# Score tiles made in pairs and one unit further ahead, in heads 1 to 7 of a first attention on TensorE

## The chip, the cores and the metric

The kernel runs on one core of a Trainium2 chip. The metric is the device time of one launch in microseconds (us). It is one fused program of two transformer blocks; the change is in the first block's attention.

## The reference, cut to what matters

```python
x = x + _L0_xattn_ref(ctx_768, _layernorm(x), mask, ...)   # the part of this case
x = x + _L0_ffn_ref(_layernorm(x), ...)
x = x + _L1_xattn_ref(_layernorm(x), ctx_768, ...)
x = x + _L1_ffn_ref(_layernorm(x), ...)                    # mixture of 8 experts
# x: 2 x 1024 x 256; context: 2 x 77 x 192; 4 heads of 64

def _L0_xattn_ref(x, latents, mask, ...):
    xn = layernorm(x); ln = layernorm(latents)
    q = ln @ Wq.T
    kv = concatenate([xn @ Wkv.T, ln @ Wlkv.T], axis=1)    # 77 + 1024 keys
    qn = rmsnorm(q) * SCALE; kn = rmsnorm(k)               # by heads
    attn = where(full_mask, einsum('bhid,bhjd->bhij', qn, kn), -max)
    out = einsum('bhij,bhjd->bhid', softmax(attn), v)
    return out @ Wo.T + bo
```

For each of 2 batches and 4 heads the scores are 1024 queries by 1101 keys, followed by a softmax over the keys, the product with the values, and the output product with Wo, which is added into x.

## The kernel before

Each engine has a program of its own, a list in fixed order written out by Python generators; semaphores are the only tie between them. The eight pairs of batch and head are heads 0 to 7. `attention(hi)` (L570) walks one head in 18 units, 9 tiles of keys (eight of 128 and one of 77) for each half of 512 queries.

For unit u TensorE makes the tile of scores (called qk here, L600 and L601: two matmuls in fp32r, the second one adding the low part and the row of maxima) in PSUM bank 4 or 5 by turns. ScalarE takes exp of it into PT[u % 4] (L1865). One unit later TensorE multiplies that by the values (pv, L583, an fp32 product that the trace shows as two matmuls) into bank 6 or 7, summed over the nine units of a half.

The softmax needs the maximum of each row first. It is made one head ahead: `max_tile(hi + 1, qt)` (L540) multiplies 128 queries by all keys into banks 0 to 2 (L547, three matmuls), and VectorE reduces all three banks to a column (L1227). After four such columns `max_row` turns them (L555), ScalarE negates them (mrt) and a DMA writes them as a row of QB. In heads 1 to 6 a max_tile stands at the end of each even unit up to 14.

The output product is made one head behind: `wo_tile(hi - 1, qt)` (L558) multiplies OT by Wo into one of banks 0 to 2, `qt % 3` (L444, which is the line of the helper `three`), and VectorE divides by the row sum (L1232) and adds into x (L1235). It stands at the end of each odd unit up to 15. Head 7 has no max_tile, only wo_tile.

`busy[m]` holds for each bank the semaphore value that frees it, and `clear(m)` waits for that. A max_tile clears banks 0, 1 and 2, so it waits for the VectorE work on the wo_tile ahead of it; a wo_tile's bank is freed by the reduction of the max_tile ahead of it. A score bank is freed by the exponential of the tile in it (`a_exp`).

After each unit the main loop (`merge`, L43) puts in side work of other stages, 1.0 or 1.4 steps a unit: query and key projections with their squares (ACT qkr, sq), transposes of a head's queries and keys (L524; ScalarE copies QA, or KA and KB; VectorE makes QB and the low half of KA), transposes of layer norms (L453), and in head 7 four small products for the feed-forward weights (L635; VectorE tsp, ScalarE w1e). These have their place in every engine's list: on ScalarE the side work after unit u - 1 comes behind exp(u - 1) and ahead of exp(u). Nothing of ScalarE's, VectorE's, GpSimd's or SyncE's lists is touched by the change. At unit 9 ScalarE and VectorE also copy the first half's result out of bank 6 (OT).

Of the kernel before, what the change touches and what calls it, by code (L numbers as in the profile page):

```python
# [82 lines left out]
def build(nc, A, out, y_dram):  # L83
    with ExitStack() as root:
# [341 lines left out]
        def tensor_program(pe):  # L426

            busy = [None] * 8
            at = {"unit": 0}
# [5 lines left out]
            def clear(b):  # L435
                if busy[b]:
                    pe.wait_ge(*busy[b])
                    busy[b] = None
# [101 lines left out]
            def max_tile(hi, qt):  # L540
                h = hi % H0
                for j in range(3):
                    clear(j)
                if qt == 0:
                    pe.wait_ge(v_ka, 2 * hi + 2)
                for j in range(3):
                    op = pe.matmul(ps[:, j, 0:368], QA[:, h, 128 * qt:128 * qt + 128], KA[:, h, 368 * j:368 * j + 368],  # L547
                                   start=True, stop=True)
                    busy[j] = (v_mx, 8 * hi + qt + 1)
                op.then_inc(p_mx, 1)  # L550

            def max_row(hi, hf):
                clear(0)
                pe.wait_ge(v_mx, 8 * hi + 4 * hf + 4)
                pe.transpose(ps[0:4, 0, 0:128], mx[:, hi % 2, 4 * hf:4 * hf + 4], ident[:, :]).then_inc(p_mT, 1)  # L555
                busy[0] = (a_mrt, 2 * hi + hf + 1)

            def wo_tile(hi, qt):  # L558
                h, m = hi % H0, qt % 3
                c = slice(128 * qt, 128 * qt + 128)  # L560
                clear(m)
                if qt % 4 == 0:
                    pe.wait_ge(v_ot, 2 * hi + qt // 4 + 1)
                if hi == 0 and qt == 0:
                    pe.wait_ge(a_whi, 3)
                    pe.wait_ge(g_wlo, 3)
                three(bank[m][:, 0:258], [((OT[0][:, c], OT[1][:, c]), (wo[0][:, h, :], wo[1][:, h, :]))]).then_inc(p_wo, 1)
                busy[m] = (v_x, 8 * hi + qt + 1)

            def attention(hi):  # L570
                b, h = HEADS[hi]
                units = [(hf, kt) for hf in range(2) for kt in range(9)]

                def pv(u):
                    hf, kt = units[u]
                    K = 128 if kt < 8 else SC
                    if kt == 0:
                        clear(6 + hf)
                    pe.wait_ge(a_exp, 18 * hi + u + 1)
                    if hf == 0 and kt == 0 and h == 0:  # L580
                        pe.wait_ge(a_v if b else v_v, 8)
                        pe.wait_ge(a_vc, b + 1)
                    pe.matmul(bank[6 + hf][0:65, :], VA[b][0:K, kt, h, :], PT[u % 4][0:K, :], start=kt == 0,  # L583
                              stop=kt == 8).then_inc(p_pv, 1)
                    if kt == 8:
                        busy[6 + hf] = (v_ot, 2 * hi + hf + 1)

                if hi == 0:
                    pe.wait_ge(g_init, 6)
                for u, (hf, kt) in enumerate(units):  # L590
                    at["unit"] = u
                    K = 128 if kt < 8 else SC
                    ks, qc = slice(128 * kt, 128 * kt + K), slice(512 * hf, 512 * hf + 512)
                    m = 4 + u % 2
                    clear(m)
                    if u == 0:
                        pe.wait_ge(v_ka, 2 * hi + 2)
                    if kt == 0:
                        pe.wait_ge(d_mrow[2 * (hi % 2) + hf], 16 * (hi // 2 + 1))
                    pe.matmul(bank[m][0:K, :], KA[:, h, ks], QA[:, h, qc], start=True, stop=False)  # L600
                    pe.matmul(bank[m][0:K, :], KB[:, h, ks], QB[:, h, qc], start=False, stop=True).then_inc(p_s, 1)  # L601
                    busy[m] = (a_exp, 18 * hi + u + 1)
                    if u:
                        pv(u - 1)
                    if hi == 0 and u < 4:
                        max_tile(0, 4 + u)
                    if hi == 0 and u == 6:
                        max_row(0, 1)
                    when = MAX_AT if hi == 0 else range(0, 16, 2)
                    if hi < 7 and u in when:  # L610
                        max_tile(hi + 1, when.index(u))
                    if hi < 7 and u == (11 if hi == 0 else 9):
                        max_row(hi + 1, 0)
                    if hi < 7 and u == 17:
                        max_row(hi + 1, 1)
                    if hi and u % 2 and u < 16:
                        wo_tile(hi - 1, u // 2)
                    yield
                pv(17)
                at["unit"] = 0  # L620
# [273 lines left out]
            for hi in range(8):  # L894
                merge(attention(hi), (beside[hi], SIDE_RATE[hi]))
                drain(beside[hi])
# [1761 lines left out]
```

## Time and profile before

| | us |
|---|---|
| median of 3 runs | 895.92 |
| lowest, highest | 895.44, 902.13 |
| profiled execution | 889.07 |
| its span, first to last instruction | 887.3 |
| TensorE busy in it | 767.5 (86%) |
| VectorE busy | 547.5 (62%) |
| ScalarE busy | 395.9 (45%) |
| granted TensorE clock, mean | 0.951 |

The profiled execution is one run of its own, a little faster than the median of the timed runs; times of single instructions are from it. Matmuls are pipelined and their ends are modelled, so the distance from one start to the next says more than a matmul's duration.

### The profile page before, as it was taken

How to read it: one execution, taken by the hardware profiler on the slowest of the kernel's cores; microseconds unless marked ns; L12 is line 12 of the kernel's file. 1: busy time of each engine (PE TensorE's matmuls, PEld its weight loads, DVE VectorE, ACT ScalarE, POOL GpSimd, SP SyncE). 2: the span in 40 equal slices, each digit the busy share in tenths (PEclk: the TensorE clock that was granted, in tenths of full speed). 3: DMA queues.
4: the chain of work that ended last, by engine and by line, in shares of the span. 5: the costliest groups of instructions: out<-in, count | busy, mean ns of one | idle time of the engine just before them, and what ended most of it. 6: DMA issues, size and time to landing. Idle time of an engine off the chain costs nothing.

```text
span 887.3 us, 12600 instructions
## 1 busy us (share of the span) xinstructions
PE 767.5 (86%) x4724; PEld 612.5 (69%) x4724; DVE 547.5 (62%) x1140; ACT 395.9 (45%) x713; POOL 346.2 (39%) x311
## 2 busy tenths in 40 slices
PE   2748998998999999997999998998128999999996
PEld 2636554665565545565977988887018999999996
DVE  5666676566477667336643349886755676765642
ACT  2324543445344433556264124443206655676562
POOL 5414200320040011215543014333422888888873
PEclk9958999999999999999999999999558999999999
DMA  6000000000000010010002020112111443455432
GB/s 177 1 0 1 1 0 1 1 1 0 2 1 1 1 48 3 1 47 2 2 1 91 1 96 1 49 49 95 48 66 30 125 120 78 108 144 141 133 38 25
DMA packets 20110, 38.38 MB, mean 43 GB/s; under 512 B 4507, under 2 KB 15633, under 8 KB 17745
## 3 DMA queue, kind: packets, MB, share of 16 engines
q1 hardware_dynamic: 13393, 29.14, 9.8%
q0 software_dynamic: 6656, 8.43, 5.3%
q8 instruction: 38, 0.62, 0.3%
q14 instruction: 23, 0.19, 0.1%
HBM read 29.02 MB, written 8.40 MB: 42 GB/s over the span
## 4 chain that ended last, share of the span: by engine, by line
PE 64%; DVE 22%; issue 5%; ACT 5%; POOL 2%; DMA 1%; ACTq 0%; DVEq 0%; POOLq 0%
PE ps L444 19%; PE ps L1060 11%; PE ps L583 9%; PE ps L683 5%; DVE mx L1227 4%; PE ps L547 3%; PE ps L600 3%; PE ps L601 2%; DVE qkn L1186 2%; PE ps L524 2%; DVE rep L1614 1%; DVE sm L1426 1%; ACT htmp L1923 1%; PE ps L453 1%; DVE Pb L1430 1%
## 5 line engine op out<-in xcount | busy, mean ns | idle before, releaser
L583 PE MATMUL ps<-PT,VA 128*65 128x512 f32 (+1 forms) x288 | 147.5, 594 | 0.2 <-ACT PT L1865 0.2
L1865 ACT ACTIVATE PT<-ps 128x512 f32<-128x512 f32 x128 | 76.0, 594 | 65.9 <-PE ps L601 65.3
L1227 DVE TENSOR_REDUCE mx<-ps 128x1 f32<-128x1104 f32 x64 | 83.5, 1304 | 34.2 <-PE ps L547 33.9
L1060 PE MATMUL ps<-he,wh 128*128 128x258 f32 x768 | 104.0, 288 | 0.0
L444 PE MATMUL ps<-GT,wh 128*128 128x258 f32 x768 | 98.0, 287 | 1.1 <-DVE GT L1703 1.1
L444 PEld LDWEIGHTS ps<-GT,wh 128*128 128x128 f32 x768 | 94.8, 192 | 1.5 <-issue 1.5
L1060 PEld LDWEIGHTS ps<-he,wh 128*128 128x128 f32 x768 | 95.4, 189 | 0.4
L2192 POOL TENSOR_TENSOR rs<-rs,half 128x4 f32<-128x4 f32 (+2 forms) x19 | 17.8, 938 | 157.5 <-DVE rs L1100 126.8
L1733 DVE TENSOR_TENSOR he<-het,he 128x516 fp32r<-128x516 f32 x64 | 44.6, 697 | 53.6 <-ACT he L1757 53.1
L2201 POOL TENSOR_TENSOR ssq<-ssq,half 128x4 f32<-128x4 f32 x32 | 32.5, 1017 | 110.8 <-DVE ssq L1168 110.6
L2466 POOL DMA_INDIRECT out_dram<-ye,idx x40 | 62.3, 1557 | 24.2 <-DVE ye L1715 14.3
L547 PE MATMUL ps<-KA,QA 128*128 128x368 f32 x192 | 61.6, 431 | 11.3 <-DVE mx L1227 3.8
L600 PE MATMUL ps<-QA,KA 128*128 128x512 f32 x144 | 68.8, 478 | 1.4 <-DMA QB<-mrt 1.4
L547 PEld LDWEIGHTS ps<-KA,QA 128*128 128x128 f32 x192 | 35.2, 198 | 46.0 <-issue 30.2
L601 PE MATMUL ps<-QB,KB 65*128 65x512 f32 x144 | 57.5, 399 | 0.0
L444 PEld LDWEIGHTS ps<-wo,OT 65*128 65x128 f32 x192 | 29.2, 189 | 40.8 <-DVE mx L1227 31.8
L583 PEld LDWEIGHTS ps<-PT,VA 128*65 128x65 f32 (+1 forms) x288 | 39.1, 138 | 24.5 <-ACT PT L1865 4.4
L2348 POOL DMA_INDIRECT gt<-y_dram,idx x40 | 41.6, 1040 | 36.6 <-DVE gate L1693 25.0
L2140 ACT ACTIVATE het<-ps,b1e 128x516 f32<-128x516 f32 x64 | 44.4, 693 | 24.5 <-PE ps L444 21.3
L683 PE MATMUL ps<-w2e,hT 128*128 128x256 f32 x384 | 51.9, 291 | 2.1 <-ACT htmp L1923 2.1
L444 PE MATMUL ps<-xt,w1e 128*128 128x512 f32 x192 | 49.7, 410 | 3.9 <-ACT htmp L1923 3.8
L683 PEld LDWEIGHTS ps<-w2e,hT 128*128 128x128 f32 x384 | 48.1, 194 | 3.9 <-ACT htmp L1923 3.0
(264 smaller groups left out, 1535.5 us busy)
## 6 DMA issues: line engine op xcount, KB each, us to landing
wr<-in_w1e_dram SPq DMA_DIRECT2D x8, 1024.0 KB, 4.8
wr<-in_w2e_dram SPq DMA_DIRECT2D x8, 1024.0 KB, 7.7
x<-in_x_dram SPq DMA_DIRECT2D x4, 512.0 KB, 7.0
w<-in_w_dram SPq DMA_DIRECT2D x2, 1024.0 KB, 4.6
y_dram<-yr SPq DMA_DIRECT2D x3, 512.0 KB, 3.0
out_dram<-x SPq DMA_DIRECT2D x3, 512.0 KB, 4.1
gt<-y_dram,idx POOLq DMA_INDIRECT x40, 3.0
out_dram<-ye,idx POOLq DMA_INDIRECT x40, 4.7
```

Source lines behind the costliest of these rows:

```text
L444: op = pe.matmul(o, l, r, start=n == 0, stop=n == len(calls) - 1)
L547: op = pe.matmul(ps[:, j, 0:368], QA[:, h, 128 * qt:128 * qt + 128], KA[:, h, 368 * j:368 * j + 368], start=True, stop=True)
L583: pe.matmul(bank[6 + hf][0:65, :], VA[b][0:K, kt, h, :], PT[u % 4][0:K, :], start=kt == 0, stop=kt == 8).then_inc(p_pv, 1)
L600: pe.matmul(bank[m][0:K, :], KA[:, h, ks], QA[:, h, qc], start=True, stop=False)
L601: pe.matmul(bank[m][0:K, :], KB[:, h, ks], QB[:, h, qc], start=False, stop=True).then_inc(p_s, 1)
L683: op = pe.matmul(bank[bk][:, 0:256], l, r, start=n == 0, stop=n == 23)
L1060: op = pe.matmul(bank[dc][:, 0:258], w2h[i][:, wc_], he[j][:, m, 258 * c:258 * c + 258], start=n == 0, stop=n == 23)
L1227: v.tensor_reduce(mx[:, hi % 2, qt:qt + 1], ps[:, 0:3, 0:368], AX.XY, ALU.max).then_inc(v_mx, 1)
L1733: v.tensor_tensor(he[1][:, m, :], het[m % 2][:, :], f(he[0][:, m, :]), ALU.subtract).then_inc(v_he, 1)
L1865: a.activation(PT[u % 4][0:K, :], bank[4 + u % 2][0:K, :], ACT.Exp, bias=0.0 if K == 128 else mcol[:, b:b + 1]).then_inc(a_exp, 1)
L2140: a.activation(het[m % 2][:, :].rearrange("p (c n) -> p c n", c=2), ps[:, bp:bp + 2, 0:258], ACT.Gelu, bias=b1e[:, ex, m:m + 1]).then_inc( ...
L2466: g_.indirect_dma_start(out, bass.IndirectOffsetOnAxis(ap=idx[0:M, ex, s_:s_ + 1], axis=0), ye[ex % 2][0:M, s_, :], None, compute_op=ALU.a ...
```

## The change

In heads 1 to 7 the tiles of scores are made two at a time. Tiles 0 and 1 are made at unit 0; in each odd unit up to 15, after pv of the unit before, come tiles u + 1 and u + 2. The order in an even unit was qk(u), pv(u - 1), max_tile and is pv(u - 1), max_tile; in an odd unit it was qk(u), pv(u - 1), wo_tile and is pv(u - 1), qk(u + 1), qk(u + 2), wo_tile. Head 0 keeps its order. The same matmuls run with the same operands and banks; only their places in TensorE's list change, and with them the places of the waits for the score banks.

```diff
-                for u, (hf, kt) in enumerate(units):
-                    at["unit"] = u
+                def qk(u):
+                    hf, kt = units[u]
                     K = 128 if kt < 8 else SC
...
                     busy[m] = (a_exp, 18 * hi + u + 1)
+
+                for u in range(18):
+                    at["unit"] = u
+                    if hi == 0:
+                        qk(u)
+                    elif u == 0:
+                        qk(0)
+                        qk(1)
                     if u:
                         pv(u - 1)
+                    if hi and u % 2 and u < 17:
+
+                        qk(u + 1)
+                        qk(u + 2)
                     if hi == 0 and u < 4:
                         max_tile(0, 4 + u)
```

## Rows read from the trace of the kernel before

**Rows 1.** The page: the first line.

```profile
span 887.3 us, 12600 instructions
```

**Rows 2.** Windows of heads 5 and 7: busy by engine (instructions), granted clock, DMA.

```profile
283.27:319.00 35.73, 35.00 (x141) 19.72 (x140) 20.78 (x36) 15.69 (x29) 0.00 (x0) 1.00 0.00 1
...
356.50:386.26 29.76, 29.60 (x106) 15.48 (x105) 9.23 (x22) 14.00 (x24) 5.11 (x4) 1.00 0.00 1
```

**Rows 3.** Waits from 66 to 387 us: us in total, times, longest.

```profile
PEld ps L444 <- DVE mx L1227: 31.8, 39, 2.2
...
PEld ps L583 <- ACT PT L1865: 4.4, 9, 0.8
```

**Rows 4.** Timeline of a plain pair in head 5: start, duration, instruction, [idle before].

```profile
297.43 0.74 PE L547 MATMUL ps<-KA,QA 128*128 128x368 f32 x3
...
298.01 0.39 PE L600 MATMUL ps<-QA,KA 128*128 128x512 f32 x1
...
298.20 1.31 DVE L1227 TENSOR_REDUCE mx<-ps 128x1 f32<-128x1104 f32 x1 [0.93 <-PE ps L547]
...
298.46 1.02 PE L583 MATMUL ps<-PT,VA 128*65 128x512 f32 x2
...
299.57 0.63 PE L444 MATMUL ps<-wo,OT 65*128 65x258 f32 x3
...
300.43 0.48 DVE L1235 SCALAR_TENSOR_TENSOR x<-ps,rec,x 128x256 f32<-128x256 f32 x1
300.51 1.02 PE L583 MATMUL ps<-PT,VA 128*65 128x512 f32 x2
...
300.97 1.07 PE L547 MATMUL ps<-KA,QA 128*128 128x368 f32 x3
...
301.88 0.39 PE L600 MATMUL ps<-QA,KA 128*128 128x512 f32 x1
...
302.34 1.02 PE L583 MATMUL ps<-PT,VA 77*65 77x512 f32 x2
```

**Rows 5.** Timeline of TensorE in head 7, one pair without side work.

```profile
368.42 1.02 PE L583 MATMUL ps<-PT,VA 128*65 128x512 f32 x2
...
369.75 1.02 PE L583 MATMUL ps<-PT,VA 128*65 128x512 f32 x2
...
370.97 0.39 PE L600 MATMUL ps<-QA,KA 128*77 128x512 f32 x1
...
371.43 1.02 PE L583 MATMUL ps<-PT,VA 128*65 128x512 f32 x2
```

**Rows 6.** Timeline of head 4 after unit 12: transposes of keys and their copies.

```profile
272.88 0.60 PE L524 MATMUL ps<-ident,qkn 128*128 128x128 f32 x4
...
273.51 0.69 ACT L1757 ACTIVATE KA<-ps,gg 128x512 fp32r<-128x512 f32 x1 [1.20 <-PE ps L524]
...
274.67 0.58 ACT L1865 ACTIVATE PT<-ps 128x512 f32<-128x512 f32 x1
...
276.46 0.78 PE L547 MATMUL ps<-KA,QA 128*128 128x368 f32 x3
```

**Rows 7.** Timeline of head 7, units 1 and 2, with side products.

```profile
358.92 0.92 PE L444 MATMUL ps<-wo,OT 65*128 65x258 f32 x3
...
359.76 0.50 PE L635 MATMUL ps<-lrow 3*128 3x256 f32 x2
...
361.79 0.58 ACT L1865 ACTIVATE PT<-ps 128x512 f32<-128x512 f32 x1
```

**Rows 8.** Timeline of head 5, unit 9 and the maximum's product after it.

```profile
303.55 0.60 PE L444 MATMUL ps<-wo,OT 65*128 65x258 f32 x3
...
305.41 0.75 PE L547 MATMUL ps<-KA,QA 128*128 128x368 f32 x3
```

**Rows 9.** Timeline of TensorE: two waits for other work, in heads 2 and 3.

```profile
183.12 0.97 PE L444 MATMUL ps<-wv,xt 128*128 128x256 f32 x6 [0.93 <-DVE OT L1241]
...
206.37 0.74 PE L547 MATMUL ps<-KA,QA 128*128 128x368 f32 x3 [0.90 <-DVE KA L1203]
```

## The prediction

> **What bounds the kernel now.** I read the windows by head first, then the waits of the first attention, then the timeline in order of time. The whole execution spans 887.3 us [rows 1] and was timed at 889.07 us, so 1.8 us lie outside the span. The change touches only heads 1 to 7 of the first attention, from 111.42 to 386.26 us of it. TensorE is the bound there, but not tight: head 5 takes 35.73 us and head 7, which makes no maxima for a later head, 29.76 us, both at a granted clock of 1.00 [rows 2]. What TensorE loses has a name: the output product (L444 of wo_tile) stands 31.8 us in 39 cases with its weight queue on the maximum (L1227) [rows 3]. That figure counts the idle weight loader, which begins long before the matmuls in front of it end, so it is no price of the wait. I take the price from one pair of units.
>
> A plain pair of head 7 has two output-of-softmax products (pv), two score tiles (qk) and one wo tile and takes 371.43 - 368.42 = 3.01 us; pv plus qk is 369.75 - 368.42 = 1.33, qk is 371.43 - 370.97 = 0.46, so pv is 0.87 and wo 3.01 - 2.66 = 0.35 [rows 5]. A plain pair of head 5 has a maximum's product more, which takes 298.01 - 297.43 = 0.58 when its bank wait is exposed and about 0.51 when not (301.88 less the end of the pv begun at 300.51) [rows 4]. So the work is 3.01 + 0.51 = 3.52 us. The pair takes 302.34 - 298.46 = 3.88 [rows 4]. The waits are thus 0.36 us a pair: the pv of 298.46 ends at 299.33, wo starts at 299.57, just after the maximum of 298.20 + 1.31 = 299.51 (0.24); the rest is its exposed weight load.
>
> Two round trips between TensorE and VectorE share banks 0 to 2 and form a ring. A, from the start of the maximum's product to the start of wo: 299.57 - 297.43 = 2.14. B, from the start of wo to the next maximum's product, which needs all three banks and so the residual add (L1235) that ends at 300.91: 300.97 - 299.57 = 1.40 [rows 4]. A + B = 3.54 cannot be undercut by any order on TensorE.
>
> **The change part by part.** *Plain pairs.* Before, both trips were covered by one qk and one pv. After, A holds pv and two qk, B only pv. A needs 0.58 + 0.87 + 0.92 = 2.37 on TensorE, more than 2.14, so the wait for the maximum goes. B has 0.35 + 0.87 = 1.22 against 1.40: a new wait of 0.18 for the residual add, on the next max_tile. The pair takes 2.37 + 1.40 = 3.77, a gain of 0.11. I count 15 pairs of this kind in the timeline (heads 1, 3, 5, 6): 1.6 us gained. What is queued behind the new wait on TensorE is the maximum's product, then pv; ScalarE's exponentials are already made and are not delayed.
>
> *The pairs at unit 9* (heads 3, 5, 6). There the residual add also stands behind the VectorE half of OT, so that B is 305.41 - 303.55 = 1.86 [rows 8], 0.18 more than the 0.35 + 0.46 + 0.87 = 1.68 that TensorE has to do in it. The two tiles now lie between pv(8) and wo, so OT is through before wo ends and B is 1.40 as elsewhere: 0.11 + 0.18, near 0.28 a pair, x 3 = 0.8 gained.
>
> *Waits from outside.* The maximum's product of head 3's first unit waits 0.90 for the keys, and a value projection 0.93 for OT [rows 9]. A score tile that was behind these waits is now before them, worth 0.46 each; two pairs of heads 2 and 4 whose wo waited 0.24 have side work in B and lose nothing there. Together 0.92 + 0.48 = 1.4 gained.
>
> *Exponentials behind side work.* This is the other side of the ledger. qk(u+2) overwrites the bank of qk(u) and so waits for exp(u). Before, a tile never waited for its bank: the pv in front of it had waited for the same exponential, and that had two qk and more in front of it (it falls short by 4.4 us in 9 cases, again by the weight loader) [rows 3]. Now exp(u) for odd u must be ready one pv and one qk after the side work of u - 1. ScalarE runs in order, and when that side work is a head's keys it copies twice before it takes the exponential. From the transposes at 272.88 the copies start at 273.51 and the exponential ends at 274.67 + 0.58 = 275.25, 2.42 after the transposes [rows 6]. TensorE has 0.35 (transposes) + 0.87 + 0.46 = 1.68 to do until then: a wait of 0.8 before the second tile. Keys fall after an even unit three times (unit 4 of heads 3 and 5, unit 12 of head 4); in head 4 the next maximum's product stood late anyway (276.46), which takes a third off. Sum 2.1 lost. After an odd unit the keys' chain also delays the maximum on VectorE, so that pv(u+1) waits 0.7 but wo comes only 0.1 to 0.2 later: four cases, 0.6. A single copy or a projection's copy and square leave 0.05 to 0.1 each, 9 cases, 0.7 lost.
>
> *Head 7.* Its units 0 to 3 carry side products whose result goes over VectorE (tsp) and ScalarE (w1e) before the next exponential. From wo at 358.92 (its matmuls run from 359.33, after the pv) the exponential of unit 2 ends at 361.79 + 0.58 = 362.37, 3.04 later [rows 7]. Before, TensorE had wo, side, qk, pv, side, qk: 0.35 + 0.35 + 0.46 + 0.87 + 0.35 + 0.46 = 2.84, nearly all of it. After, wo, side, pv, side: 1.92, a wait of 1.1. The same after unit 3 without the second side product gives 1.5, and the tile after unit 0's side waits 0.75. That is 3.35; before, the covers of 2.84 and, after unit 3, 2.49 fell short of 3.04 too, by 0.2 and 0.55, so 2.6 are lost anew. The rest of head 7 has no wait before and gets none. If the side results came 1 us sooner, no more than 0.8 would be lost.
>
> Instructions added: none. The unit 0 of the next head has its row from the DMA some ten units early, and qk(9), now made at unit 7, needs a row sent at unit 17 of the head before; no queue is passed.
>
> Sum: -1.6 - 0.8 - 1.4 + 2.1 + 0.6 + 0.7 + 2.6 = +2.2 us against the profiled execution's 889.07, which is 891.3. The median of the three runs is 895.92; by ratio (1.0025) that becomes 898.2.
>
> A rule weighed: the row shows the exponential of the keys' unit 2.42 us after the transposes, against 1.68 us of cover [rows 6]. The Trainium skill, Perfetto Trace Analysis, "Matmuls", says that independent groups should rotate through different PSUM banks so that one is emptied while the next is made; two tiles back to back over only two banks leave that rotation. By it every pair would pay; by the rows only those with side work on ScalarE do, since in a plain pair the exponential ends over 1 us before its bank is wanted.
>
> **The rivals.** *The wait goes and nothing takes its place.* If the residual add came back faster than 1.40, all 0.36 of 18 pairs would go (6.5), and the outside waits 1.4: about 888. For it: the change aims at just this wait, the largest of TensorE's here [rows 3]. Against: B is the end of a matmul, a reciprocal and an add of 0.48 us in a row, which the change doesn't touch, and the cover of 1.22 is counted from the same rows [rows 4, 5].
>
> *Exponentials bind everywhere that side work is* (the slower side). Its place is the second tile's bank wait, its price up to 0.8 for each of the ten double copies of keys in heads 1 to 5, and 2.6 in head 7; it decides once ScalarE's in-order side copy ends later than one pv and one qk after its product. That is 8 + 2.6 + 1.3 less the 3.8 gained: +8, and with each projection's copy at 0.15 more, +10: 906. For it: ScalarE's queue is strictly ordered in the rows [rows 6, 7]. Against: half of the copies fall on odd units, where VectorE's chain hides them.
>
> *It does nothing:* VectorE's own chains (norms, the products that scale queries and keys) set most of the odd pairs, and gains and losses cancel: 896.
>
> *The clock falls.* The granted clock is 1.00 in these heads in spite of idle stretches [rows 2]; waits of 1.5 us in head 7 are new. At half clock for the first third of that head it would take about 10 us more: 908. The Trainium skill, TensorE: Matmul & The Clock Gate, "A second HAM failure mode", tells of a kernel whose short idles between groups made the clock oscillate; no row of this stretch shows that.
>
> **How the numbers follow.** Forecast (a few us slower, mostly given back) 0.66; exponentials bind 0.13; the wait simply goes 0.11; nothing 0.08; clock 0.02. A change of 1% (9 us) is about what a measurement of this kernel can tell, its three runs lying 6.7 us apart. The range of the forecast alone is 893 to 903: B between 1.22 and 1.45, and keys' waits between 0.3 and 1.0. To the rivals it is 888 to 906. Faster by over 1% needs more than the whole of the first rival: 0.07. Slower by over 1% is the upper part of the second and the clock: 0.11. Within 1%: 0.82.
>
> **What would show it.** Right: the weight loader's wait of L444 for L1227 shrinks to a third, that of L547 for L1235 grows to over 5 us; plain pairs of head 5 at 3.77; a new wait of L600 for an exponential in heads 3, 4, 5, 7; head 7 near 32 us, heads 3 to 6 within 1 us of before. Wrong: plain pairs at 3.55 (first rival), a wait before every second tile (second), or head 7 unchanged, which would take away my largest loss and leave the kernel at 896 or below.

## The result, and the profile after

The changed kernel takes 904.30 us, median of 20 runs (901.76 to 913.81); the kernel before 898.01 us, median of 20 (892.04 to 906.77; the three runs known before the prediction are among them). The ratio is 1.0101 with a 95% interval of 1.0078 to 1.0124: about 9 us slower. The ratio leaves out three slow, disturbed runs, all of the kernel before, and mostly for that reason is larger than the distance of the two medians (6.3 us). The profiled execution after took 903.53 us, that of before 889.07.

The page of the changed kernel, first line and granted clock in 40 slices:

```profile
span 901.7 us, 12600 instructions
...
PEclk9968999799999999999999999999558999999999
```

No instruction was added. I cut the span at the turning of the maxima (L555) in unit 17 of each head, which both kernels have, and measured from one to the next; head 7 ends at the first matmul of the experts. Times in us, with the clock where it is not 1.00:

| stretch | before | after | difference |
|---|---|---|---|
| start to head 0's turning | 110.85 (0.89) | 114.02 (0.88) | +3.2 |
| head 1 | 40.24 | 41.05 | +0.8 |
| head 2 | 52.35 | 56.59 (0.91) | +4.2 |
| head 3 | 37.07 | 36.71 | -0.4 |
| head 4 | 42.19 | 44.26 | +2.1 |
| head 5 | 35.72 | 35.59 | -0.1 |
| head 6 | 37.50 | 36.65 | -0.9 |
| head 7 | 30.34 | 32.59 | +2.2 |
| rest (experts and so on) | 501.04 (0.94) | 504.24 (0.94) | +3.2 |

The two outer stretches hold none of the change, since head 0 keeps its order, and they differ as much between executions of one order: over the twelve experiments below the first is 110.8 to 114.8 and the last 499.7 to 513.8. They are left out of the account, which is therefore one of the heads alone. The changed heads cost 8.0 us: 4.2 in head 2, 4.3 in heads 4 and 7, 0.8 in head 1, less 1.3 in heads 3, 5 and 6.

The heads of the changed kernel as windows (busy by engine with instructions, granted clock, DMA), heads 2, 4, 5 and 7; the last two answer to [rows 2]:

```profile
155.07:211.66 56.59, 52.12 (x238) 34.53 (x237) 31.06 (x59) 21.94 (x54) 13.74 (x13) 0.91 0.00 1
...
248.37:292.63 44.26, 40.76 (x189) 25.89 (x187) 30.83 (x54) 19.50 (x44) 11.87 (x10) 1.00 0.00 1
292.63:328.22 35.59, 34.66 (x141) 20.22 (x140) 20.95 (x36) 14.87 (x28) 0.00 (x0) 1.00 0.00 1
...
364.87:397.46 32.59, 30.19 (x109) 15.93 (x107) 9.39 (x22) 13.45 (x25) 5.11 (x4) 1.00 0.00 1
```

Head 2 is the only head with a clock under 1.00, and it is the largest loss. Where in it? The timeline of TensorE, changed kernel, around the end of head 1 (start, duration, instruction, [idle before]):

```profile
153.36 1.88 PE L583 MATMUL ps<-PT,VA 128*65 128x512 f32 x4
155.07 0.27 PE L555 MATMUL ps<-ident,mx 128*4 128x128 f32 x1
156.87 0.26 PE L469 MATMUL ps<-ident,yb 77*128 77x77 f32 x1 [1.52 <-DVE yb L1153]
156.96 0.23 PE L470 MATMUL ps<-ident,yb 77*64 77x77 f32 x1
157.63 1.99 PE L475 MATMUL ps<-wc,ctxT 128*77 128x512 f32 x2 [0.44 <-ACT ctxT L1769]
159.55 1.99 PE L476 MATMUL ps<-wc,ctxT 64*77 64x512 f32 x2
161.46 1.97 PE L583 MATMUL ps<-PT,VA 77*65 77x512 f32 x2
```

and the same place in the kernel before:

```profile
152.14 0.26 PE L469 MATMUL ps<-ident,yb 77*128 77x77 f32 x1 [0.78 <-DVE yb L1141]
...
152.90 1.08 PE L475 MATMUL ps<-wc,ctxT 128*77 128x512 f32 x2 [0.44 <-ACT ctxT L1757]
153.91 1.08 PE L476 MATMUL ps<-wc,ctxT 64*77 64x512 f32 x2
154.92 1.07 PE L583 MATMUL ps<-PT,VA 77*65 77x512 f32 x2
```

Here TensorE turns (transposes) the second batch item's normalised context (yb) and multiplies it into keys and values. The norm comes from VectorE, whose program the change does not touch. Before, units 16 and 17 still had a tile of scores each to put in front of it; now both tiles were made at unit 15, only pv products are left, and the wait is 1.52 us, not 0.78. From L475 on the same matmuls take nearly twice as long: the engine stood, did 0.3 us of small transposes, stood again, and then had its clock halved. In windows of 6 us the changed kernel reads

```profile
149.00:155.00 6.00, 5.98 (x25) 3.16 (x24) 4.76 (x11) 3.82 (x6) 0.02 (x1) 1.00 0.00 0
155.00:161.00 6.00, 4.05 (x8) 0.83 (x6) 1.08 (x3) 0.61 (x3) 0.53 (x1) 0.71 0.00 0
161.00:167.00 6.00, 6.00 (x16) 4.00 (x16) 2.51 (x5) 1.84 (x4) 1.40 (x2) 0.50 0.01 3
167.00:173.00 6.00, 6.00 (x33) 4.53 (x33) 2.75 (x6) 2.41 (x7) 1.01 (x1) 0.93 0.00 0
```

0.50 is the 1.2 GHz level, 1.00 the 2.4 GHz level; 6 us at 0.50 hold 16 instructions, and 6 us just behind hold 33. Before, the windows from 152 to 164 us are at 1.00. The wait itself costs 0.7 us and the clock some 4.

The waits of the weight loader in the first attention after (us in total, times, longest), which answer to [rows 3]:

```profile
PEld ps L600 <- ACT PT L1877: 11.3, 28, 1.0
PEld ps L547 <- DVE x L1247: 11.1, 17, 1.9
PEld ps L583 <- ACT PT L1877: 8.6, 11, 2.0
...
PEld ps L444 <- DVE mx L1239: 2.4, 5, 1.4
```

### The profile page after: what moved, and what is told of

Read it like the earlier page. It is cut to its first block, busy times and chain, and to the rows that moved or that the text cites. A ratio compares the mean times of both kernels' runs of the same rounds, so it can differ in the third digit from the quotient of the medians.

```text
span 901.7 us, 12600 instructions
## 1 busy us (share of the span) xinstructions
PE 774.2 (86%) x4724; PEld 617.3 (68%) x4724; DVE 551.2 (61%) x1140; ACT 390.9 (43%) x713; POOL 346.8 (38%) x311
## 4 chain that ended last, share of the span: by engine, by line
PE 65%; DVE 20%; ACT 6%; issue 5%; POOL 2%; DMA 1%; another core or an unknown queue 0%; ACTq 0%; DVEq 0%; POOLq 0%
PE ps L444 19%; PE ps L583 10%; PE ps L1072 9%; PE ps L695 5%; PE ps L547 4%; PE ps L600 3%; PE ps L601 3%; DVE qkn L1198 2%; DVE mx L1239 2%; PE ps L524 2%; DVE rep L1626 1%; DVE yb L1116 1%; DVE sm L1438 1%; ACT htmp L1935 1%; PE ps L453 1%
## 5 line engine op out<-in xcount | busy, mean ns | idle before, releaser
L444 PE MATMUL ps<-GT,wh 128*128 128x258 f32 x768 | 97.9, 287 | 1.1 <-DVE GT L1715 1.1
L444 PEld LDWEIGHTS ps<-GT,wh 128*128 128x128 f32 x768 | 94.7, 192 | 1.5 <-issue 1.5
L600 PE MATMUL ps<-QA,KA 128*128 128x512 f32 x144 | 86.3, 599 | 3.5 <-ACT PT L1877 2.0
L1877 ACT ACTIVATE PT<-ps 128x512 f32<-128x512 f32 x128 | 72.8, 591 | 36.7 <-PE ps L601 36.6
L547 PEld LDWEIGHTS ps<-KA,QA 128*128 128x128 f32 x192 | 34.6, 201 | 51.8 <-issue 27.4
L547 PE MATMUL ps<-KA,QA 128*128 128x368 f32 x192 | 57.8, 411 | 12.9 <-DVE x L1247 4.6
L444 PE MATMUL ps<-xt,w1e 128*128 128x512 f32 x192 | 49.9, 411 | 4.2 <-ACT htmp L1935 4.2
L583 PEld LDWEIGHTS ps<-PT,VA 128*65 128x65 f32 (+1 forms) x288 | 36.8, 139 | 21.2 <-issue 9.3
L600 PEld LDWEIGHTS ps<-QA,KA 128*128 128x128 f32 x144 | 27.0, 188 | 32.3 <-issue 18.7
```

Source lines behind the costliest of these rows:

```text
L444: op = pe.matmul(o, l, r, start=n == 0, stop=n == len(calls) - 1)
L1877: a.activation(PT[u % 4][0:K, :], bank[4 + u % 2][0:K, :], ACT.Exp, bias=0.0 if K == 128 else mcol[:, b:b + 1]).then_inc(a_exp, 1)
```

## Experiments

Twelve kernels ran, in four groups (1 to 4, 5 to 7, 8 to 10, 11 and 12). Each ratio is to the kernel before as timed in the same group; its own median moved between 891.0 and 900.3 us from group to group, so only ratios are compared across groups. The heads (from turning to turning, as above) in each one's profiled execution, in us, and where the granted clock was below 1.00:

| kernel | h1 | h2 | h3 | h4 | h5 | h6 | h7 |
|---|---|---|---|---|---|---|---|
| before | 40.24 | 52.35 | 37.07 | 42.19 | 35.72 | 37.50 | 30.34 |
| after | 41.05 | 56.59 (.91) | 36.71 | 44.26 | 35.59 | 36.65 | 32.59 |
| 1 head1_old | 40.23 | 52.02 | 36.68 | 44.31 | 35.63 | 36.60 | 32.56 |
| 2 filler_ctx | 41.05 | 52.71 | 36.65 | 44.31 | 35.64 | 36.61 | 35.76 (.90) |
| 3 before_tail1 | 40.23 | 56.84 (.91) | 37.07 | 42.19 | 35.73 | 37.55 | 30.33 |
| 4 pairs_again | 41.05 | 56.57 (.91) | 36.67 | 44.25 | 35.65 | 36.68 | 32.57 |
| 5 head7_old | 41.06 | 52.75 | 36.67 | 44.27 | 35.63 | 38.15 (.96) | 30.33 |
| 6 one_ahead | 40.02 | 54.42 (.94) | 36.61 | 42.65 | 35.51 | 37.05 | 30.95 |
| 7 chosen_heads | 40.22 | 52.03 | 36.04 | 45.23 (.96) | 34.66 | 38.14 (.96) | 30.31 |
| 8 chosen_2 | 40.23 | 52.01 | 36.02 | 42.16 | 34.66 | 37.05 | 30.33 |
| 9 chosen_2_filled | 40.23 | 51.92 | 36.02 | 42.17 | 34.66 | 37.06 | 30.32 |
| 10 before_filled | 40.26 | 52.30 | 37.07 | 42.19 | 35.66 | 37.52 | 30.35 |
| 11 tail1_again | 40.28 | 56.79 (.91) | 37.07 | 42.19 | 35.68 | 37.53 | 30.34 |
| 12 tail1_filled | 40.27 | 53.04 | 37.07 | 42.18 | 35.67 | 37.45 | 30.34 |

At full clock one order gives the same head within 0.1 us in every execution, so a head's own cost can be read from a single profile.

**1. head1_old: head 1 keeps the old order.**

```diff
-                    if hi == 0:
+                    if hi in (0, 1):
...
-                    if hi and u % 2 and u < 17:
+                    if not (hi in (0, 1)) and u % 2 and u < 17:
```

> The changed kernel, but head 1 keeps the old order (as head 0 does). Theory (tail and clock): in the changed kernel TensorE has no score tiles left to do while VectorE and GpSimd prepare the context's key projection at the end of head 1; it stands 1.5 us, and the granted clock is at half until some 10 us later. With head 1 in the old order the clock stays at 1.00 between heads 1 and 2 and the stretch from the turning of the last maxima of head 0's successor (L555) to that of head 2 returns to the 52.4 us of before: 3.5 to 5.5 us faster than the changed kernel in this stretch, about 1.005 of the kernel before in all. Rival (exponentials behind side work cost most): head 1 holds only two or three such places, so at most 1 us faster than the changed kernel.

902.76 us against 897.58, ratio 1.0036 [0.9999, 1.0072]. As expected, the wait for yb is 0.78 again, the clock stays at 1.00, and heads 1 and 2 take 92.25 us together, 5.4 less than in the changed kernel and 0.3 less than before.

**2. filler_ctx: the changed order, with work in front of the two waits.** Seven matmuls into a free bank ahead of the wait for yb, two ahead of that for ctxT; nobody reads them.

```diff
+                if b:
+                    clear(2)
+                    for _ in range(7):
+                        pe.matmul(bank[2], KA[:, 0, 0:128], QA[:, 0, 0:512], start=True, stop=True)
                 pe.wait_ge(v_cz, b + 1)
```

> The changed kernel with nine matmuls without a reader (512 columns, bank 2) at the end of head 1: seven ahead of the wait for the normed context (v_cz), two ahead of the wait for its copy (a_cT). They fill the time in which TensorE stands. Theory (clock): the work added costs 1.9 us of TensorE, most of it in time that is idle anyway, and the granted clock stays at 1.00 there, so it is 2 to 4 us FASTER than the changed kernel though it does more. Rival (no clock effect, only order): 0 to 1.5 us slower than the changed kernel.

901.48 us against 897.58, ratio 1.0053 [1.0011, 1.0094]. Head 2 is at full clock in this execution. But head 7 lost 3.2 us to the clock instead, at its own new waits (0.53 us and the 0.72 below). Three other executions with the same order in head 7 (after, experiments 1 and 4) did not fall there. TensorE there:

```profile
364.31 1.07 PE L591 MATMUL ps<-PT,VA 128*65 128x512 f32 x2
...
366.54 1.97 PE L591 MATMUL ps<-PT,VA 128*65 128x512 f32 x2 [0.72 <-ACT PT L1885]
```

**3. before_tail1: the order of before, with only head 1's last two tiles made at unit 15.**

```diff
...
+                    if not (hi == 1 and u > 15):
+                        qk(u)
...
                     if u:
                         pv(u - 1)
...
+                    if hi == 1 and u == 15:
+                        qk(16)
+                        qk(17)
```

> The kernel before, with one change: in head 1 tiles 16 and 17 are made together at unit 15. Theory (tail and clock): these two tiles are all that covered the context's chain, so this alone costs 3 to 5 us against the kernel before and shows the granted clock at half at the end of head 1. Rival (the pairs in the body of the heads cost): no change within 1 us, granted clock 1.00.

902.92 us against 897.58, ratio 1.0051 [1.0008, 1.0095]. Moving two tiles of heads 1 to 7's 126 makes head 2 take 56.84 us, all of the changed kernel's loss there and a little more. The first transpose, and then the window around it, with the clock at 0.69:

```profile
153.41 0.26 PE L469 MATMUL ps<-ident,yb 77*128 77x77 f32 x1 [1.52 <-DVE yb L1149]
```

```profile
152.00:158.00 6.00, 4.15 (x7) 0.83 (x7) 1.08 (x3) 0.54 (x3) 0.08 (x1) 0.69 0.00 0
```

**4. pairs_again: the changed kernel once more.** No edit.

> The changed kernel once more, as the reference of this call and to see whether its clock falls in the same place. Theory: 1.008 to 1.012 of the kernel before, granted clock at half from about 45 us into head 1 for some 10 us. Rival (the fall was chance): no fall there, 1.004 to 1.006.

910.53 us in 4 runs, ratio 1.0115 [1.0054, 1.0177]. Head 2 is the same to 0.02 us.

**5. head7_old: head 7 keeps the old order**, as in experiment 1 with `(0, 7)`.

> The changed kernel, but head 7 keeps the old order. Theory (exponentials behind side work): from the last L555 to the first product of the feed-forward layer it takes 30.3 us again against 32.6 in the changed kernel, and the kernel is 2.3 us or more faster than the changed one; the granted clock of that stretch is 1.00. Rival (the pairs cost nothing in head 7, only the clock does): the stretch stays at 32.6.

897.23 us against 891.78, ratio 1.0054 [1.0025, 1.0083]. Head 7 is back at 30.33. One thing speaks against a simple story of head 1: this kernel has the same end of head 1 as the changed one, with the same two waits, and the clock did not fall.

```profile
153.65 0.26 PE L469 MATMUL ps<-ident,yb 77*128 77x77 f32 x1 [1.52 <-DVE yb L1153]
...
154.41 1.08 PE L475 MATMUL ps<-wc,ctxT 128*77 128x512 f32 x2 [0.44 <-ACT ctxT L1769]
```

So the long wait makes the fall possible, not certain, and filler_ctx alone proves little. That is why experiments 11 and 12 were made. It also gives the price of the fall with nothing else changed: head 2 takes 52.75 us here and 56.59 in the changed kernel.

In head 6, however, the clock fell to 0.96, and it took 38.15 us instead of 36.65. Its maximum's product waits for a residual add, 1.53 us in the order of before and 1.98 in pairs, since the score tile in front of it is gone too:

```profile
336.75 0.74 PE L547 MATMUL ps<-KA,QA 128*128 128x368 f32 x3 [1.98 <-DVE x L1247]
```

**6. one_ahead: one tile further ahead, but no pairs.** Tiles 0 and 1 at unit 0, then pv(u - 1) and qk(u + 1) in every unit.

```diff
...
-                    if hi and u % 2 and u < 17:
-
+                    if hi and 0 < u < 17:
                         qk(u + 1)
-                        qk(u + 2)
```

> Heads 1 to 7 with one tile a unit, made one unit further ahead: pv(u-1), qk(u+1), then max_tile or wo_tile. It takes the lead from the change without the pair. Theory: both trips between TensorE and VectorE have one tile and one pv as before, so plain pairs of units stay at 3.85 to 3.9 us and heads 5 and 6 gain nothing (35.7 and 37.5 us); no tile waits for its bank; but the end of head 1 lacks a tile, the context's chain stands longer and the granted clock falls there, so the stretch from head 1's last L555 to head 2's takes 54 to 57 us against 52.4. Rival (the lead alone pays, by earlier exponentials): heads 5 and 6 shorter by over 0.5 us.

894.27 us against 891.78, ratio 1.0022 [0.9996, 1.0049]. A plain pair takes 3.86 us (pv at 313.99 to pv at 317.85), as before the change; heads 4 and 7 lose 0.5 and 0.6 where the pairs lose 2.1 and 2.2. What remains of the loss is mostly head 2 (+2.1), where the wait for yb is 1.26 and the clock fell for a shorter time.

**7. chosen_heads: pairs only where the rows of the first runs gave a gain.** `PAIRS[hi]` lists the units at which two tiles are made; a tile that no pair has made is made in its own unit, as before.

```diff
+PAIRS = ((), (), range(-1, 16, 2), range(7, 16, 2), range(-1, 10, 2), range(7, 16, 2), range(-1, 16, 2), ())
```

> Pairs only where the traces show a gain: all of heads 2 and 6, from unit 7 on in heads 3 and 5 (behind the side work on keys), up to unit 9 in head 4; the old order in heads 1 and 7 and at the end of head 4. Theory: a plain pair of units takes 3.67 us against 3.88, so heads 3 and 5 come to 35.9 and 34.7 us (37.1 and 35.7 before, 36.7 and 35.6 in the changed kernel), head 6 to 36.6, head 2 to 52.0, head 4 to 42.0 to 42.5 against 44.3 since the tail of its key work is covered again: 2.5 to 3.5 us less than the kernel before, 0.996 to 0.998 of it in the timed runs, granted clock 1.00 in all heads. Rival (the lead costs wherever it is taken up): heads 3 and 5 gain less than 0.3 us and head 4 stays over 43.5.

894.25 us against 891.78, ratio 1.0020 [0.9994, 1.0045]: not the gain that was expected. Heads 3 and 5 gained as planned; head 4 lost 3 us, and head 6 came to 38.14, with the same wait (1.99) and the same fall to 0.96 as in experiment 5. In its unit 11 a maximum is late in every kernel; before, TensorE stood 1.33 us for it at full clock. With the pairs ended just ahead of it there was less in front. TensorE's timeline:

```profile
271.91 0.84 PE L446 MATMUL ps<-wo,OT 65*128 65x258 f32 x3 [1.91 <-DVE mx L1243]
272.56 0.84 PE L526 MATMUL ps<-ident,qkn 128*128 128x128 f32 x3
```

and the window behind it, with a granted clock of 0.72:

```profile
272.00:278.00 6.00, 6.00 (x23) 4.09 (x23) 2.64 (x4) 2.29 (x4) 0.00 (x0) 0.72 0.00 0
```

The same fault in two other heads: a tile moved away from in front of a wait that other work sets.

**8. chosen_2: head 4 in the old order, in head 6 no pair at unit 5.**

```diff
+PAIRS = ((), (), range(-1, 16, 2), range(7, 16, 2), (), range(7, 16, 2), (-1, 1, 3, 7, 9, 11, 13, 15), ())
```

> As the kernel with chosen heads, but head 4 in the old order throughout and head 6 without the pair at unit 5, so that no pair runs ahead of a long VectorE product on which TensorE must wait. Theory (a pair in front of a long wait lengthens the idle stretch and risks the clock): head 4 takes 42.2 us and head 6 36.9 to 37.2 us with the granted clock at 1.00; heads 3 and 5 stay at 36.0 and 34.7; the kernel is 2 to 3 us below the kernel before, 0.996 to 0.999. Rival: the falls come by chance wherever TensorE waits, and the kernel is at 1.000 or above.

893.34 us against 900.34, ratio 0.9919 [0.9883, 0.9955]: faster than before, by more than the 0.1 to 0.4% that were expected, and by its ratio faster than the changed kernel, which was not timed beside it. The heads came out as expected, without a fall.

**9. chosen_2_filled** has twelve added matmuls in front of four long waits as well (3 and 1 at the context's, 4 at head 4's unit 11, 4 at head 6's unit 6).

```diff
+                    if hi == 4 and u == 11:
+                        fill(4, 4)
+                    if hi == 6 and u == 6:
+                        fill(5, 4)
```

> The same with matmuls that nobody reads, in the three longest idle stretches of this attention: four at the end of head 1, four before wo_tile at unit 11 of head 4, four before the maximum's product at unit 6 of head 6. Theory (clock): no fall in heads 1 to 7 in the profile and in most runs, 3 us or more below the kernel before (0.994 to 0.998), and no slower than the one without them by more than 0.5 us. Rival: the filling only delays, 0.5 to 1 us slower than without it.

891.76 us (6 runs), ratio 0.9897 [0.9845, 0.9949]. Its interval and that of chosen_2 overlap, so that the fillers help is not shown by the pair. The gain is again larger than expected.

**10. before_filled: the same twelve matmuls in the order of before.**

> The kernel before with the same twelve matmuls and nothing else. Theory (clock): they lie in idle time, so the heads take what they took (within 0.3 us) and the runs are 0 to 2 us faster on average, since now and then a fall is spared: 0.997 to 1.000. Rival: 0.5 to 1 us slower.

895.96 us against 900.34, ratio 0.9955 [0.9915, 0.9995], though no head differs from before by over 0.1 us. What it gains lies outside the heads or in falls of the clock that this one execution doesn't show. With the same fillers in both orders, the chosen pairs are 4.2 us faster (891.76 against 895.96) and their heads 3.0 us shorter, which fits better than the 7.3 us of experiment 8.

**11 and 12. tail1_again, tail1_filled: experiment 3 once more, and with the nine matmuls of experiment 2 in it.** The edits are those shown above.

> The order of before with only the last two tiles of head 1 made two units earlier, once more. Theory (the tail of head 1 is cover for the context chain, and without it the granted clock may fall): the first transpose of the context waits 1.52 us as in the first run of this kernel; where the clock falls behind it, head 2 takes 56.8 us, otherwise 52.7; in executions with the long wait it fell in three of four so far, so the median is 2 to 5 us above the kernel before, ratio 1.002 to 1.006. Rival (the fall is chance and has nothing to do with the tail): ratio 1.000, head 2 at 52.3 to 52.7.

> The same order of head 1's tail, with seven matmuls of 512 columns that nobody reads ahead of the wait for the context's norm and two ahead of the wait for its copy, so that TensorE stands at neither. No part of the reference is left out. Theory: the clock stays at 1.00 behind the context, head 2 takes 52.7 us, and the kernel is at 1.000 to 1.002 of before, 2 to 4 us faster than the same order without the added matmuls in the same call. Rival: the work moved costs by itself, whatever the clock; then both kernels have the same ratio.

Without the added matmuls 895.16 us, ratio 1.0035 [1.0011, 1.0059]; with them 891.89, ratio 1.0015 [0.9991, 1.0039], both against 891.01. The profile without them, and then the one with them:

```profile
153.57 0.26 PE L469 MATMUL ps<-ident,yb 77*128 77x77 f32 x1 [1.52 <-DVE yb L1149]
...
154.33 1.99 PE L475 MATMUL ps<-wc,ctxT 128*77 128x512 f32 x2 [0.44 <-ACT ctxT L1765]
```

```profile
151.40 1.85 PE L471 MATMUL ps<-QA,KA 128*128 128x512 f32 x7
153.08 0.28 PE L473 MATMUL ps<-ident,yb 77*128 77x77 f32 x1
...
153.23 0.71 PE L479 MATMUL ps<-QA,KA 128*128 128x512 f32 x2
153.87 1.08 PE L483 MATMUL ps<-wc,ctxT 128*77 128x512 f32 x2
```

The chain itself is no shorter: from the first transpose to the first product are 0.76 and 0.79 us. TensorE is merely busy while it waits, and head 2 takes 53.04 us in place of 56.79. In the median of ten runs the difference is 3.3 us; the intervals of the two ratios overlap, but nine of the ten runs without the added matmuls took over 892.62 us and only one of the ten with them.

Counting all profiled executions at the end of head 1: with the wait at 1.52 the clock fell in four of five (after, 3, 4 and 11, not 5); at 1.26 once, for a shorter time (6); at 0.78 or 0.79 in none of four (before, 1, 7, 8); with the tiles gone but nine matmuls put in their place, in neither of two (2, 12). Experiments 9 and 10 kept the tiles there and say nothing on it. Two executions are few for a fall that also stayed away once without them; that the idle time is the cause rests on all these rows and the timed runs together.

## Why the prediction was wrong

The forecast was 898.2 us, 2.3 above the median before, with slower by over 1% at 0.11. The direction came out as forecast and the size did not. By its own steps:

**The clock, the step that failed.** The sum has no term for it. The rival "the clock falls" named the right mechanism, but at head 7, where it came in one of four executions and cost 3.2 us and not about 10, and gave it 0.02, because the granted clock was 1.00 in all heads in spite of idle stretches [rows 2]. That looked at waits that the change makes through banks and exponentials. It didn't look at waits that other work sets, once the tiles in front of them are gone. The step "waits from outside" did ask that, but only in one direction: it counted a tile that comes before such a wait (heads 2 and 3, a gain) and not the tiles that leave the end of a head. Measured in place of nothing: 3.8 us of clock in head 2 (56.59 less 52.75, experiment 5; 3.75 between experiments 11 and 12), in four of five executions, and 1.5 us in head 6 in two of six. The Trainium skill, TensorE: Matmul & The Clock Gate, "A second HAM failure mode", which the prediction set aside since no row showed it, speaks of frequent short idles between groups of matmuls, from cycling through banks, that make the clock go to and fro. The rows here agree only in part: short idles do lower the clock, but these are two idles at one place, set by another engine's chain, and the clock falls once. The same page, "What's actually happening", says that how many slow matmuls a kernel starts with varies from run to run; that is about a kernel's start, and the four falls in five executions with the same wait show a variation of this kind in the middle of one.

**Head 4, mis-sized.** The terms for head 4 come to some 0.8 us (a keys' wait, odd units); it lost 2.1. The wait of the second tile is there (0.50, below), but two others were not counted. The maximum's product in unit 6 waits 1.09 for the residual add where it waited 0.35. And the lead is not given back at the end: the transposes of the last keys now stand behind two tiles and wo, and the last pv waits for the copies and exponentials that follow them:

```profile
266.08 0.75 PE L547 MATMUL ps<-KA,QA 128*128 128x368 f32 x3 [1.09 <-DVE x L1247]
...
284.14 0.50 PE L600 MATMUL ps<-QA,KA 128*128 128x512 f32 x1 [0.50 <-ACT PT L1877]
...
289.29 0.60 PE L524 MATMUL ps<-ident,qkn 128*128 128x128 f32 x4
...
289.93 0.69 ACT L1769 ACTIVATE KA<-ps,gg 128x512 fp32r<-128x512 f32 x1 [1.58 <-PE ps L524]
...
291.56 0.68 ACT L1877 ACTIVATE PT<-ps,mcol 77x512 f32<-77x512 f32 x1
291.72 1.07 PE L583 MATMUL ps<-PT,VA 128*65 128x512 f32 x2 [0.97 <-ACT PT L1877]
```

In the old order the head is at 42.16 again (experiment 8). TensorE's idle time in the head went from 42.19 - 40.16 = 2.03 to 44.26 - 40.76 = 3.50 us, with the late maximum of unit 11 down from 1.33 to 0.94. That the loss is these waits is read from the rows; they were not tried one by one.

**Plain pairs, right and a little better.** Forecast 3.77 against 3.88 before. After, in head 5:

```profile
308.78 0.75 PE L547 MATMUL ps<-KA,QA 128*128 128x368 f32 x3
309.36 1.02 PE L583 MATMUL ps<-PT,VA 128*65 128x512 f32 x2
...
311.15 0.52 PE L444 MATMUL ps<-wo,OT 65*128 65x258 f32 x3
...
311.91 0.48 DVE L1247 SCALAR_TENSOR_TENSOR x<-ps,rec,x 128x256 f32<-128x256 f32 x1
312.45 0.77 PE L547 MATMUL ps<-KA,QA 128*128 128x368 f32 x3
```

A is 311.15 - 308.78 = 2.37, the forecast figure; B is 312.45 - 311.15 = 1.30 and not 1.40, since the loader no longer waits for the maximum: it starts on wo's weights at 310.92, while the tile in front still runs, and wo's matmuls take 0.52 against 0.63 in [rows 4]. So B is not fixed by VectorE alone, and the prediction's floor of 3.54 for A + B does not hold. The pair takes 3.67. The loader's wait of L444 for the maximum, 31.8 us in 39 cases [rows 3], is 2.4 in 5, far less than the third that was forecast, and that of L547 for the residual add is 11.1; over 5 was forecast. Removing the kernel's largest named wait was worth about 0.2 us a pair, because B took its place. one_ahead shows that making tiles in pairs does this: one tile ahead without it leaves the two units at 3.86. The pair at unit 9 takes 316.32 - 312.45 = 3.87; in head 5 before it took 4.12, so 0.25 is gained where 0.28 was forecast. No second tile of a plain pair waits for its bank, so of the two readings weighed in the prediction that of the rows held.

**Waits from outside, gained and given back.** The two gains of 0.46 are there: the wait of the value projection for OT is gone, and that of head 3's maximum's product for the keys is 0.38 where it was 0.90. But a wait just ahead of the second, for kc at the end of head 2, lost its own tile and went from 0.95 to 1.46, and the waits for the residual add in heads 2 and 6 grew by 0.45 each. No 1.4 us were gained: heads 2 and 3 are each about 0.3 us shorter at full clock (52.02 in experiment 1, 36.71).

```profile
210.31 0.65 PE L524 MATMUL ps<-ident,qkn 128*128 128x128 f32 x4 [1.46 <-DVE kc L1220]
...
214.60 0.75 PE L547 MATMUL ps<-KA,QA 128*128 128x368 f32 x3 [0.38 <-DVE KA L1215]
```

**Keys' exponentials, right kind, two thirds of the size.** The new waits of L600 for an exponential stand where forecast, in heads 3, 4, 5 and 7, at 0.50 to 0.52 where about 0.8 was. Heads 3, 5 and 6 are within 1 us of before, as forecast; head 4, of which the same was said, is not.

```profile
PE ps L600 <- ACT PT L1877: 2.0, 4, 0.5
```

Where the first units of heads 3 and 5 keep the old order and pairs begin behind the keys, the gain rises from 0.4 and 0.1 to 1.05 and 1.06 (experiment 8), so the early pairs cost those heads 0.69 and 0.93, their own gains already taken off.

**Head 7, right.** Forecast +2.6, measured +2.25 (head near 32: 32.59), and head7_old takes it back whole. TensorE's waits after:

```profile
369.36 0.50 PE L600 MATMUL ps<-QA,KA 128*128 128x512 f32 x1 [0.52 <-ACT PT L1877]
...
373.03 1.07 PE L583 MATMUL ps<-PT,VA 128*65 128x512 f32 x2 [0.73 <-ACT PT L1877]
...
377.99 1.07 PE L583 MATMUL ps<-PT,VA 128*65 128x512 f32 x2 [1.15 <-ACT PT L1877]
```

0.75, 1.1 and 1.5 had been forecast for the three.

**Heads 1 and 2 without the clock.** Head 1 was forecast with a small gain and took 0.8 more; with head 2 at full clock (experiment 5) the two come to 93.81 against 92.59. Since head 1 in the old order puts both back to 92.25 (experiment 1), the 1.2 to 1.6 us belong to head 1's order and the longer wait at its end; the part of each is open.

The account: the heads' 8.0 us are 3.8 of clock and 4.2 of order. The order's part is nearly twice the forecast +2.2, with head 4, head 1 and the outside waits mis-sized. The timed 9.1 us (interval 7.0 to 11.1) agrees with 8.0, though the stretches outside the heads vary by more than the distance. That the kernel became slower was forecast for the waits of heads 4 and 7, which came; nearly half of the loss is a mechanism that the sum did not have.

**What stays open.** chosen_2 is 7.3 us faster by the timed runs (interval 4.1 to 10.5), while its heads save 2.95 us in the profile. In that group the median run of the kernel before had a mean granted clock of 0.941 and that of chosen_2 0.945; how often the clock falls seems to differ also outside the heads (before_filled points there too), and no experiment settles where.

## What to carry to other kernels

Before work is made earlier, ask what it stood in front of: at the end of a loop it is the cover for chains of other engines, and with it gone a wait of 0.8 us became 1.5 and then, in most executions, cost 4 us of clock. So price every existing outside wait twice, with the cover that leaves it and with the cover that comes to it. A wait between two engines that share banks is half of a ring: removing it is worth only the distance to the other half, here 0.2 of 0.36 us a pair. And making tiles early paid here only where ScalarE, which works in order, had no side work behind them, so choose the places by head. One profile at full clock does not clear a wait: the same program fell in one execution and not in another.

## What the runs showed of the hardware

The granted clock went to the 1.2 GHz level behind two idles of 1.5 and 0.4 us with 0.3 us of small transposes between, in four of five executions, and stayed low for some 10 us although TensorE was busy throughout from the first product on. Idles of 0.78 and 0.44 at the same place did it in none of four. A single idle of 1.91 in head 4 did it in its one execution, and one of 1.98 in head 6 in two of six; one of 1.33 in head 4, of 1.53 in head 6 or of 1.46 in head 2 never did. Length alone does not decide, since in head 7 the clock fell once in four behind idles of 0.53 and 0.72. In both executions in which nine matmuls that nobody reads (1.85 and 0.71 us of TensorE) stood in the long wait the clock stayed up, and they cost nothing on the path. The last 500 us, with the same instructions in every kernel, differ by up to 14 us between executions, so a change in the heads of a few us is read better from the heads' rows than from one time.
